# One last stage of a three-stage kernel: two PE turnings become DMA transposes, and work changes its place in the turn

## The reference

```
h = einsum('bhid,oi,od->bho', x, weighted_sum, weight)          # stage 1
h = concat([h, txt], axis=1)
h = h + attention(layernorm(h))                                 # stage 2, attends over the batch axis
h = h + ffn(layernorm(h))                                       # stage 3, the last one
# ffn, for each row t (x is the normalised row, H = 16 heads, E = 8 experts):
q   = rmsnorm(x) @ Wq + bq                      # [16 heads, 16]
kv  = (rmsnorm(x) @ Wdown + bdown) @ Wup + bup
att = softmax(q k^T / 4) ; out = att v          # attention of the 16 heads of one row with each other
x2  = x + out @ Wo + bo
h2  = rmsnorm(x2) ; gate = softmax(h2 @ Wg + bg)
y   = x2 + sum_e gate_e * (h2 @ We_e)           # all 8 experts
```

## Time and profile before

| | us |
|---|---|
| median of 3 runs (lowest, highest) | 804.05 (800.21, 805.13) |
| profiled execution, its own time | 801.38 |
| its span, first to last instruction | 799.3 |
| PE busy, share of the span | 745.6, 93% |
| DVE busy | 703.5, 88% |
| ACT, POOL busy | 374.4 (47%), 409.4 (51%) |
| mean granted clock of TensorE | 0.981 |

### The profile page before, as it was taken

How to read it: one execution, slowest core, us unless ns; L and a number is a source line. 1 busy time by engine, 2 the same in 40 slices (tenths; PEclk the granted TensorE clock), 3 DMA queues, 4 the chain that set the end, 5 groups by cost and what they waited for, 6 DMA issues and landing times.

```text
span 799.3 us, 48197 instructions
## 1 busy us (share of the span) xinstructions
PE 745.6 (93%) x20274; PEld 508.0 (64%) x20274; DVE 703.5 (88%) x1591; ACT 374.4 (47%) x985; POOL 409.4 (51%) x1094
## 2 busy tenths in 40 slices
PE   4999978999999999876999999999999999999997
PEld 3888855666666666654656666666666666666553
DVE  5798778999999999765799999999999999999987
ACT  4478544665566665543333443344344434343321
POOL 1231355555666667444455665566556655665411
PEclk9999999999999999987899999999999999999999
DMA  9987000000000000000011001100111011101100
GB/s 331 326 252 228 3 3 4 2 0 0 0 0 0 0 0 2 11 17 10 15 26 28 23 16 26 26 23 16 26 26 26 14 26 26 26 13 27 29 16 20
DMA packets 38377, 33.25 MB, mean 42 GB/s; under 512 B 24786, under 2 KB 33570, under 8 KB 38314
## 3 DMA queue, kind: packets, MB, share of 16 engines
q1 hardware_dynamic: 38314, 32.35, 13.4%
HBM read 22.64 MB, written 4.83 MB: 34 GB/s over the span
## 4 chain that ended last, share of the span: by engine, by line
PE 39%; DVE 10%; issue 3%; DVEq 0%
PE bank L204 9%; PE bank L205 8%; PE bank L206 8%; PE bank L957 5%; PE bank L946 5%; DVE acc L1099 3%; DVE smax L1108 2%; PE bank L964 1%; DVE res L1099 1%; PE bank L977 1%; PE bank L1016 1%; PE bank L1003 1%; PE bank L1002 1%; DVE fq_t L1147 1%; DVE logits L1117 1%
## 5 line engine op out<-in xcount | busy, mean ns | idle before, releaser
L1099 DVE SCALAR_TENSOR_TENSOR acc<-bank,gate,acc 128x256 f32<-128x256 f32 x222 | 106.1, 478 | 12.8 <-PE bank L206 4.1
L204 PE MATMUL bank<-we_h,h_t_h 128*128 128x512 f16 x296 | 113.0, 382 | 3.7 <-DVE res L1099 1.0
L205 PE MATMUL bank<-we_l,h_t_h 128*128 128x512 f16 x296 | 112.2, 379 | 0.6 <-issue 0.6
L206 PE MATMUL bank<-we_h,h_t_l 128*128 128x512 f16 x296 | 112.2, 379 | 0.0
L204 PE MATMUL bank<-tokw_h,x_t_h 128*128 128x256 f16 x256 | 71.0, 277 | 11.3 <-DVE x_t_l L682 11.3
L1053 ACT ACTIVATE junk<-x 128x256 f32<-128x256 f32 x37 | 15.4, 417 | 120.4 <-DVE x L1143 120.4
L205 PE MATMUL bank<-tokw_l,x_t_h 128*128 128x256 f16 x256 | 70.9, 277 | 0.0
L206 PE MATMUL bank<-tokw_h,x_t_l 128*128 128x256 f16 x256 | 70.8, 277 | 0.0
L1188 POOL TENSOR_TENSOR t<-ss,rms_ws 128x1 f32<-128x1 f32 x37 | 7.1, 192 | 117.1 <-ACT junk L1053 117.1
L287 PE MATMUL bank<-vaug,pr_t 32*32 32x17 f32 x4736 | 49.8, 181 | 10.7 <-issue 10.7
L957 PEld LDWEIGHTS bank<-pr_t,v 32*32 32x32 f32 x4736 | 47.6, 104 | 18.7 <-issue 18.3
(11 more groups left out here) (223 smaller groups left out, 2232.8 us busy)
## 6 DMA issues: line engine op xcount, KB each, us to landing
xbuf<-in_x SPq DMA_DIRECT2D x32, 512.0 KB, 5.3
out<-res SPq DMA_DIRECT2D x36, 128.0 KB
we_s<-in_we SPq DMA_DIRECT2D x4, 512.0 KB, 7.3
inw<-in_in_w SPq DMA_DIRECT2D x1, 768.0 KB, 11.6
hn_t_h<-hn_r_h SPq DMA_TRANSPOSE x37, 2.3
hn_t_l<-hn_r_l SPq DMA_TRANSPOSE x37, 2.4
wrep<-in_w_rep SPq DMA_DIRECT2D x1, 512.0 KB, 4.8
h_all<-in_txt SPq DMA_DIRECT2D x1, 512.0 KB
```

The costliest lines, as they stand in the source:

```text
L204: nc.tensor.matmul(dst, a_h(c), b_h(c), start=start and c == 0, stop=False)
L205: nc.tensor.matmul(dst, a_h(c), b_l(c), start=False, stop=False)
L206: last = nc.tensor.matmul(dst, a_l(c), b_h(c), start=False, stop=stop and c == chunks - 1)
L1099: op = nc.vector.scalar_tensor_tensor(out=(res if e == E - 1 else acc)[:, :], in0=b_we[s % 2][:, k * D:(k + 1) * D], scalar=gate[p][:, e:e ...
```

## The change

`fon` and `x2` are now split as they lie and turned by DMA, as `hn` already was. ACT copies `fon` to `on_r_h` and `x2` to `x2_r_h`; POOL subtracts `on_r_l` at the head of its turn; DVE subtracts `x2_r_l`, both operands from SBUF, behind `v`. SP issues six DMA transposes for a turn. PE's four turning matmuls are gone. `wo` moves behind the sums, and the gate logits behind q. On DVE `fq_t` now stands ahead of `x2`. On POOL `hn_r_l` (now of the tile whose rows ACT wrote in the turn before) and the coefficients move from the end of the turn to behind `lat_l`, except in the filling turns.

```diff
@@ -832,6 +832,8 @@
...
         hn_r = halves("hn_r", [P, D])
+        on_r = halves("on_r", [P, D])
+        x2_r = halves("x2_r", [P, D])
         fq_t = sb("fq_t", [P, 32, H])
@@ -964,36 +966,21 @@
...
                     scores(range(0, 16)).then_inc(f_s, 1)
-                if real(i, -2):
-                    pe.wait_ge(f_h2l, i - 1)
-                    wait(pe, f_x2, i - 1)
-                    rows_times(b_gate, *h2_t[p], lambda c: wg_h[:, c, :], lambda c: wg_l[:, c, :]).then_inc(f_gate, 1)
-                if real(i, -1):
-                    pe.wait_ge(f_on, i)
-                    wait(pe, f_h2l, i - 1)
-                    if isinstance(i, int) and i == 1:
-                        pe.wait_ge(a_sub, TILES)
-                    for c in range(KC):
-                        last = nc.tensor.transpose(b_turn[:, c * P:(c + 1) * P],
-                                                   fon[:, :, :].rearrange("p h d -> p (h d)")[:, c * P:(c + 1) * P],
-                                                   ident[:, :])
-                    last.then_inc(f_onps, 1)
                 if real(i, 1):
...
                                lambda c: wq_l[:, c, :]).then_inc(f_q, 1)
+                if real(i, -2):
+                    pe.wait_ge(x2_in, 32 * (i - 1))
+                    wait(pe, f_x2, i - 1)
+                    rows_times(b_gate, *h2_t[p], lambda c: wg_h[:, c, :], lambda c: wg_l[:, c, :]).then_inc(f_gate, 1)
                 experts(i, p, 0)
...
                 experts(i, p, 1)
-                if real(i, -1):
-                    pe.wait_ge(f_onl, i)
-                    wait(pe, f_logit, i - 1)
-
-                    rows_times(b_wo, fon_h, fon_l, lambda c: wo_h[:, c, :], lambda c: wo_l[:, c, :]).then_inc(f_wo, 1)
                 if middle:
@@ -1009,12 +996,12 @@
...
                     sums(range(0, 16), p).then_inc(f_av, 1)
+                if real(i, -1):
+                    pe.wait_ge(on_in, 32 * i)
+                    wait(pe, f_logit, i - 1)
+
+                    rows_times(b_wo, fon_h, fon_l, lambda c: wo_h[:, c, :], lambda c: wo_l[:, c, :]).then_inc(f_wo, 1)
                 experts(i, p, 2)
-                if real(i, -1):
-                    pe.wait_ge(f_x2, i)
-                    for c in range(KC):
-                        last = nc.tensor.transpose(b_turn[:, c * P:(c + 1) * P], x2[:, c * P:(c + 1) * P], ident[:, :])
-                    last.then_inc(f_h2ps, 1)
                 experts(i, p, 3)
@@ -1022,9 +1009,9 @@
...
                 if real(i, -1):
-                    act.wait_ge(f_onps, i)
-                    wait(act, f_wo, i - 1)
-                    nc.scalar.activation(fon_h[:, :, :], b_turn[:, 0:D], ACT.Copy).then_inc(f_onh, 1)
+                    act.wait_ge(f_on, i)
+                    wait(act, on_in, 32 * (i - 1))
+                    nc.scalar.activation(on_r[0][:, :], fon[:, :, :], ACT.Copy).then_inc(f_onh, 1)
                 if real(i, 1):
@@ -1049,6 +1036,8 @@
...
                     act.wait_ge(f_x2, i)
+                    wait(act, x2_in, 32 * (i - 1))
+                    nc.scalar.activation(x2_r[0][:, :], x2[:, :], ACT.Copy).then_inc(f_x2h, 1)
                     wait(act, p_t2, i - 1)
@@ -1060,11 +1049,6 @@
...
                                          scale=cf_all[:, at, RS:RS + 1].squeeze(1)).then_inc(f_x1, 1)
-                if real(i, -1):
-                    act.wait_ge(f_h2ps, i)
-                    wait(act, f_gate, i - 2)
-                    wait(act, f_we, (i - 2) * STEPS)
-                    nc.scalar.activation(h2_t[1 - p][0][:, :, :], b_turn[:, 0:D], ACT.Copy).then_inc(f_h2h, 1)
                 if real(i, 3):
@@ -1123,9 +1107,6 @@
...
                     nc.vector.transpose(pr_t[1][:, :, :], pr[:, :, :]).then_inc(f_prt, 1)
-                if real(i, -1):
-                    dve.wait_ge(f_onh, i)
-                    nc.vector.tensor_tensor(fon_l[:, :, :], b_turn[:, 0:D], fon_h[:, :, :], ALU.subtract).then_inc(f_onl, 1)
                 if real(i, -2):
@@ -1134,17 +1115,17 @@
...
                 combine(i, p, 1)
+                if real(i, 1):
+                    dve.wait_ge(f_qpad, i + 2)
+                    nc.vector.transpose(fq_t[:, :, :].rearrange("r t h -> r h t"), qpad[:, :, :])
                 if real(i, -1):
...
                     wait(dve, f_ss2, i - 1)
-                    wait(dve, f_h2ps, i - 1)
                     nc.vector.scalar_tensor_tensor(out=x2[:, :], in0=b_wo, scalar=1.0 / WS, in1=x1b[:, :],
...
                 if real(i, 1):
-                    dve.wait_ge(f_qpad, i + 2)
-                    nc.vector.transpose(fq_t[:, :, :].rearrange("r t h -> r h t"), qpad[:, :, :])
                     dve.wait_ge(f_kv, i + 2)
@@ -1152,6 +1133,10 @@
...
                                         kv_t[:, :, :].rearrange("r g (p t) -> r p g t", t=2)).then_inc(f_qt, 1)
+                if real(i, -1):
+                    dve.wait_ge(f_x2h, i)
+                    wait(dve, x2_in, 32 * (i - 1))
+                    nc.vector.tensor_tensor(x2_r[1][:, :], x2[:, :], x2_r[0][:, :], ALU.subtract).then_inc(f_x2l, 1)
                 if middle:
@@ -1160,20 +1145,31 @@
...
                     nc.vector.reciprocal(frsum[:, :], of[:, :, HD:HD + 1]).then_inc(f_rsum, 1)
-                if real(i, -1):
-                    dve.wait_ge(f_h2h, i)
-                    nc.vector.tensor_tensor(h2_t[1 - p][1][:, :, :], b_turn[:, 0:D], h2_t[1 - p][0][:, :, :],
-                                            ALU.subtract).then_inc(f_h2l, 1)
                 if real(i, 0):
                     dve.wait_ge(f_rsum, i + 1)
-                    wait(dve, f_onps, i)
+                    wait(dve, p_onl, i)
                     nc.vector.tensor_tensor(fon[:, :, :], of[:, :, 0:HD], frsum[:, :].unsqueeze(2).to_broadcast([P, H, HD]),
...
         def ffn_pool(pool):
+            def low(j):
+
+                pool.wait_ge(f_hn, j + 1)
+                nc.gpsimd.tensor_tensor(hn_r[1][:, :], hn[:, :], hn_r[0][:, :], ALU.subtract).then_inc(p_hnl, 1)
+
+            def coefs(i):
+
+                if real(i, AHEAD) and real(i, 0):
+                    ffn_coefficients(pool, i + AHEAD)
+
             def body(i, p):
+                filling = isinstance(i, int) and i <= 0
+                if real(i, -1):
+                    pool.wait_ge(f_onh, i)
+                    nc.gpsimd.tensor_tensor(on_r[1][:, :], fon[:, :, :].rearrange("p h d -> p (h d)"), on_r[0][:, :],
+                                            ALU.subtract).then_inc(p_onl, 1)
                 if real(i, 1):
@@ -1183,6 +1179,10 @@
...
                     nc.gpsimd.tensor_tensor(lat_l[0:LAT, :], lat[:, :], lat_h[0:LAT, :], ALU.subtract).then_inc(p_latl, 1)
+                if real(i, 2) and not filling and not (isinstance(i, int) and i == 1):
+                    low(i + 2)
+                if not filling:
+                    coefs(i)
                 if real(i, -1):
@@ -1197,11 +1197,10 @@
...
                     nc.gpsimd.tensor_tensor(x1b[:, :], x1[:, :], bo_s[:, :], ALU.add).then_inc(p_x1, 1)
-                if real(i, 3):
-                    pool.wait_ge(f_hn, i + 4)
-                    nc.gpsimd.tensor_tensor(hn_r[1][:, :], hn[:, :], hn_r[0][:, :], ALU.subtract).then_inc(p_hnl, 1)
-                if real(i, AHEAD) and real(i, 0):
-                    ffn_coefficients(pool, i + AHEAD)
+                if filling:
+                    if real(i, 3):
+                        low(i + 3)
+                    coefs(i)
 
@@ -1247,18 +1246,34 @@
...
             def _(sp):
-                for i in range(TILES + 4):
-                    if i < TILES:
-                        sp.wait_ge(f_hn, i + 1)
-                        wait(sp, f_down, i)
+                for i in range(-2, TILES + 3):
+                    if real(i, -1):
+                        sp.wait_ge(f_onh, i)
+                        wait(sp, f_wo, i - 1)
+                        wait(sp, on_in, 32 * (i - 1))
+                        sp.dma_start_transpose(fon_h[:, :, :], on_r[0][:, :]).then_inc(on_in, 16)
+                        sp.wait_ge(p_onl, i)
+                        sp.dma_start_transpose(fon_l[:, :, :], on_r[1][:, :]).then_inc(on_in, 16)
+                    if real(i, 2):
+                        sp.wait_ge(f_hn, i + 3)
+                        wait(sp, f_down, i + 2)
                         sp.dma_start_transpose(hn_h[:, :, :], hn_r[0][:, :]).then_inc(hn_in, 16)
-                        sp.wait_ge(p_hnl, i + 1)
+                        sp.wait_ge(p_hnl, i + 3)
                         sp.dma_start_transpose(hn_l[:, :, :], hn_r[1][:, :]).then_inc(hn_in, 16)
-                    if i >= 4:
-                        at = (i - 4) * P
+                    if real(i, -3):
+                        at = (i - 3) * P
                         rows = min(P, TOKENS - at)
-                        sp.wait_ge(f_comb, (i - 3) * STEPS)
+                        sp.wait_ge(f_comb, (i - 2) * STEPS)
```

(9 more changed lines are left out.)

8 lines of the change are left out of this document (4 added, 4 removed).

## The result

The changed kernel takes **821.09 us** (median of 4 runs, 818.94 to 827.28) against 804.59 us for the kernel before on the same chip: 1.0237 times as long, 95% interval 1.0194 to 1.0279 (the ratios here are those on record, which need not be the quotient of the two medians, here 1.0205). So the change costs some 16 to 19 us. The forecast was 807 us with a range of 796 to 816: too low, and the result lies outside the range.

The account below looks back on a forecast made before the run. DVE's own list of operations was taken to set the stage 3 turn. 31 turns x 0.08 us plus 3.3 us for the ends gave +5.8 on the profiled 801.4 us: 807 us, range 796 to 816.

Parts of the forecast that it names:

- DVE's list: DVE operations in a steady turn: `fon_t_l` gone -0.31 us, `h_t_l` gone -0.16, `x2_r_l` added +0.36.
- The gate: Small DVE operation in each steady turn: held until POOL's `hn_r_l` ends, +0.3 us, against -0.08 as `qpad` leaves.
- The bound of 0: Lower bound on the gate's added time: no cost if issued some hundredths ahead of `hn_r_l`; upper bound 0.67 us.
- The two meet: DVE reaches `x2` at 6.93 to 7.10 us, PE's `wo` is ready at 6.98: at most +0.05, taken 0.02.
- rival A: Gate slips through in steady turns, DVE's list shrinks, PE's pause goes: 799.4 us; chance 0.25.
- Power on POOL: Power `r2` on POOL beside DVE's `x2_r_l`: does not hold DVE once it has read, cost 0.02 us.
- Rival C: Power, or two POOL instructions, holds `x2_r_l`: +0.5 us each turn, 822 us, or 815 without the gate; chance 0.11.
- Six transfers: Six DMA transposes on SP each turn: they fit, land 2.4 us after issue and cost nothing.
- The front: First turns of stage 3: `wo` and `x2` stand behind the sums, PE half idle: 0, give or take 1 us.
- The end: Last turns of stage 3: latency from `x2` to gate matmul unhidden, 4.5 us instead of 2.20: +3.3 us together.

Follow-up runs that it names:

- e1_low_early: Changed kernel with POOL's `hn_r_l` moved ahead of `lat_l`, right behind `qpad`, nothing else: 819.43 us, ratio 1.0181.
- e5_load: Kernel before plus four spare transposing transfers a turn that nobody reads, with the transfer of `res` one queue round later: 802.62 us, ratio 1.0002.
- e12_mid_only: Changed kernel with `wo` put back between kv and the sums on PE, nothing else: 808.92 us, ratio 1.0107.
- e6_wo_late: Kernel before with `wo` moved behind the sums and `fq_t` ahead of `x2`, both turns still on PE: 820.81 us, ratio 1.0231.
- e2_x2_pe: Changed kernel with `x2` turned by PE again, `fon` still by transposing transfers: 809.33 us, ratio 1.0079.
- e11_again: Changed kernel once more, unaltered, for a second profile and more runs: 819.92 us, ratio 1.0224.
- e8_wo_mid: Changed kernel with `hn_r_l` ahead of `lat_l`, `wo` between kv and the sums, and `x2` turned by PE: 795.49 us, ratio 0.9913.
- e4_spare: Kernel before plus four spare transposing transfers a turn, with the transfer of `res` left in its old place in SP's queue: 884.13 us, ratio 1.1001.
- e9_low_mid: Changed kernel with `hn_r_l` ahead of `lat_l` and `wo` between kv and the sums, `x2` still turned by transfers: 800.14 us, ratio 1.0001.

## Why the prediction was wrong

Two terms for the ends failed, the front above all, and the gate was taken too small. By the prediction's own steps, with mean offsets of the turns that start between 470 and 700 us in each kernel:

- **DVE's list, right.** `fon_t_l` gone: -0.31 (said -0.31). `h_t_l` gone: -0.16 (-0.16). `x2_r_l` holds its place for 0.30, and the operation behind it takes 0.03 longer: 0.33, between the lower bound of 0.31 and the 0.36 of the sum.
- **The gate, right in mechanism, small in size.** From the gate's start to the next operation DVE took 0.47 us before and 0.75 after, +0.28; I had summed +0.25 - 0.08. The turn is +0.17, not +0.08: 3 us of the miss. The bound of 0, "if the gate is issued some hundredths ahead of `hn_r_l`", does not exist in this order: it is issued so in every second turn, `lat_l` is still running then, and the gate is held until `hn_r_l` ends.
- **"The two meet", wrong in size.** PE's step 1 to the end of `wo` was taken as 3.83 us, from the order before. In the new order the sums stretch to 1.58 us, and `x2` could start at 7.20, not 6.98 (`e1_low_early`). The held gate put `x2` at 7.25, only 0.05 us behind this bound. So rival A (gate free, turn 11.21) could not come true by the gate alone; it came true with `wo` ahead of the sums (11.20).
- **Power on POOL, right.** In 13 of the 26 turns from 442 to 750 us the power `r2` began 0.08 to 0.09 us ahead of `x2_r_l` (578.47 and 578.56 in the rows of after); `x2_r_l` took 0.38 us all the same. In the other 13 both began within 0.02 us, and the power took 0.80 instead of 0.55: there it was POOL that was held. Rival C, 31 x 0.5 us, did not come. The Trainium skill, SBUF — State Buffer, "SBUF: two separate sides", where whichever starts first gets the port pair "for the whole instruction", is not borne out for a power (the words I quoted for it, "held for the full instruction", stand in that page's Terms): by it `x2_r_l` would have been held until the power's end, some 0.46 us later, in the first 13.
- **Six transfers, right in steady turns** (landing 2.3 and 2.4 us after issue, turn unharmed by load in `e5_load`).
- **The front, "0, give or take 1": the step that failed.** It cost 6 us (turns 0 to 6: 82.9 and 81.6 us, before 76.3). I argued that PE is half idle there and did not look at PE's rows of these turns. They show, before, a stall of 1.38 us in the sums with `wo` ahead of it. The change moves `wo`, and `x2` with it, behind that stall and behind kv, and DVE waits for `wo` in three turns, 8.9 us in all. (PE also waits twice for x2's transfers there, 2.0 us in all; `e12_mid_only` keeps 1.8 us of that.) With `wo` moved back (`e12_mid_only`) the six turns take 75.0 us; with that move alone made in the kernel before (`e6_wo_late`), 82.6. Two things stay open: how much of the 6 us is the granted clock, which is 0.84 in these turns and 0.90 before, and why `e2_x2_pe` gets most of it back with `wo` behind the sums.
- **The end, mis-sized.** The round trip itself was right: x2 at 800.10 to the gate's product at 804.64 is 4.54 us (said 4.5). But PE waits for x2's transfers four times, 6.9 us in all, not once and a bit; a stall stands ahead of `wo` here too, and `x2` waits 1.96 us behind it; and the clock falls to half behind some of the stops. With `wo` ahead of the sums the end costs 3.7 us (`e12_mid_only`), near the 3.3 of the sum: what the sum lacked is what the transfers cost together with `wo`'s new place. Said +3.3, measured 8 to 10.

Sum of the misses: 3 in the steady turns, 6 at the front, 5 to 6 at the end, that is 14 to 15 us, on a forecast of 807: 821 to 822. The parts are read from one profile of before and two of after. The waits for `wo` at the front are named by my own last sentence ("a turn in which DVE waits for PE's `wo`"), but without a price and without a rival of its own.

## What to carry to other kernels

A steady turn (one in the middle of the stage, where each repeats the last) says little about the turns at either end: read the waiting engine's rows there too, and look for stalls that cost nothing only because nobody stands behind them. Before moving a product behind a long run of small ones, list who waits for it. Where two bounds lie within 0.3 us, price the edit against the second: the repairs were worth 1 and 11 us alone and 20 together.

## What the runs showed of the hardware

- The run of 128 small products on PE, or the product just behind it, is held up by a stall of 1.1 to 2.3 us in turn 2 of every kernel, with or without the extra transfers, in some also in turn 4 or 5 (at 415.08 us before, 1.21; at 431.12 in `e11_again`, 2.10) and in turn 35 (after, 1.79; before none). Between 442 and 750 us neither before, after nor `e8_wo_mid` has one. The profile gives only "issue" as their cause. In the kernel, turns 4 to 33 are a loop over two turns and the others are written out, so all these stalls lie where PE runs a piece of its list for the first time. Whether that is the cause is not tested.
- The sums lasted 1.22 us in 19 of 20 turns of `e5_load`, 1.34 in the kernel before with the same instructions on PE, and 1.57 in all profiles of after. Neither the load (1.22 with it) nor the place behind or ahead of `wo` (1.36 and 1.42 behind it) explains this. It stays open.
- Four more transposing transfers a turn cost nothing by their load (`e5_load`, 1.0002) and 82 us by their place in SP's queue (`e4_spare`).
- Four stops of PE of 1.2 to 2.2 us at the end went with a granted clock of 0.88 in a window; in `e9_low_mid` three such stops, 4.1 us, and in `e12_mid_only` three, 4.8 us, left it at 1.00 from 750 to 790 us. What decides is not shown.
- A POOL operation with two operands in SBUF held a 128x8 operation of DVE until its own end (0.51 us at least instead of 0.29, after); with `hn_r_l` moved away the same operation took 0.29 in all 27 turns (`e9_low_mid`). A power on POOL did not hold a DVE subtraction of two SBUF operands: 0.38 us in the 13 turns in which the power began 0.08 to 0.09 us ahead, and 0.38 us in the 13 in which both began together (after).
